# An adaLN transformer block: the gates go to rows through memory, and batch 1 is turned in periods 6 and 8

## The reference

```python
mod = (_silu(c) @ wmod).reshape(2, 6, 1, -1)
sa, ca, ga, sb, cb, gb = (mod[:, i] for i in range(6))
ga = (2 * (ga >= 0) - 1) * jnp.maximum(jnp.abs(ga), 0.25)
gb = (2 * (gb >= 0) - 1) * jnp.maximum(jnp.abs(gb), 0.25)
h = _layernorm(x) * (1 + ca) + sa
x = x + ga * attention(h)          # q, k, v; rope; causal softmax; Wo
h = _layernorm(x) * (1 + cb) + sb
x = x + gb * experts(h)            # top 2 of 8, rank-16 LoRA on w1, w3, w2
```

## Time and profile before

| | us |
|---|---|
| median of three runs | 471.87 (469.65 to 472.2) |
| time of the profiled execution | 469.36 |
| its span, first to last instruction | 467.6 |

### The profile page before, as it was taken

One profiled execution on the slowest core, in us unless ns is written; L12 is line 12 of the kernel. 1 busy time (PEld: TensorE's weight loads), 2 busy tenths in 40 slices (PEclk: granted clock), 3 DMA queues, 4 the chain that ended last, 5 costly groups with the idle time before them and its releaser, 6 DMA issues.

```text
span 467.6 us, 12314 instructions
## 1 busy us (share of the span) xinstructions
PE 438.4 (94%) x4511; PEld 314.3 (67%) x4511; DVE 364.2 (78%) x1004; ACT 349.1 (75%) x640; POOL 338.3 (72%) x287
## 2 busy tenths in 40 slices
PE   7978999989999999999999998988899997899995
PEld 4455776877877788787788876877765454454563
DVE  5975988888888789888889898988756669445576
ACT  3656999989899899989989889889626465653351
POOL 5448699996799976769999869935315875375792
PEclk8997999999999999999999999999999999999999
DMA  8347344765132774334357424491110000000001
GB/s 294 114 140 240 106 101 130 173 176 163 42 114 52 189 173 127 99 80 126 96 157 160 120 61 114 70 199 30 35 35 0 2 0 1 1 2 0 24 22 47
DMA packets 57948, 44.60 MB, mean 95 GB/s; under 512 B 36832, under 2 KB 49568, under 8 KB 57888
## 3 DMA queue, kind: packets, MB, share of 16 engines
q1 hardware_dynamic: 57472, 43.28, 34.8%
q10 hardware_dynamic: 416, 0.53, 0.3%
HBM read 23.41 MB, written 11.53 MB: 75 GB/s over the span
## 4 chain that ended last, share of the span: by engine, by line
PE 61%; ACT 12%; DVE 10%; POOL 8%; issue 6%; DMA 1%; ACTq 0%; DVEq 0%; POOLq 0%
PE ps L558 10%; PE ps L474 8%; PE ps L476 8%; PE ps L475 8%; PE ps L539 5%; PE ps L541 5%; PE ps L582 3%; ACT prob L962 3%; PE ps L586 3%; PE ps L584 3%; ACT ph L969 3%; PE ps L797 2%; PE ps L771 2%; DMA oT<-wmod 1%; POOL wst L1654 1%
## 5 line engine op out<-in xcount | busy, mean ns | idle before, releaser
L1306 DVE CUSTOM_DVE_ANT_0 prob<-ps,causal 128x512 f32<-128x512 f32 (+3 forms) x256 | 117.9, 485 | 11.5 <-PE ps L541 9.6
L962 ACT ACTIVATE prob<-prob,least 128x512 f32<-128x512 f32 (+3 forms) x256 | 122.6, 556 | 2.7 <-DVE least L1306 2.7
L1314 DVE SCALAR_TENSOR_TENSOR pl<-ps,ph 128x512 f16<-128x512 f32 (+1 forms) x128 | 105.1, 821 | 23.7 <-ACT ph L969 20.2
L969 ACT ACTIVATE ph<-ps 128x512 f16<-128x512 f32 (+1 forms) x128 | 87.1, 703 | 24.5 <-PE ps L558 21.9
L539 PE MATMUL ps<-kT_h,qT 128*128 128x512 f16 (+3 forms) x256 | 76.8, 302 | 7.9 <-DVE least L1306 5.4
L558 PE MATMUL ps<-ident,prob 128*128 128x128 f32 x640 | 82.6, 276 | 1.1 <-DVE pl L1314 0.6
L558 PEld LDWEIGHTS ps<-ident,prob 128*128 128x128 f32 x640 | 69.6, 142 | 2.4 <-DVE pl L1314 1.1
L541 PE MATMUL ps<-kT_l,qT 128*128 128x512 f16 (+3 forms) x256 | 70.4, 302 | 0.0
L582 PE MATMUL ps<-vh,ph 128*128 128x65 f16 x640 | 64.9, 194 | 2.5 <-ACT hT L913 1.2
L584 PE MATMUL ps<-vl,ph 128*128 128x64 f16 x640 | 64.9, 193 | 0.0
L586 PE MATMUL ps<-vh,pl 128*128 128x65 f16 x640 | 64.8, 193 | 0.0
(11 more groups left out here) (195 smaller groups left out, 1013.6 us busy)
## 6 DMA issues: line engine op xcount, KB each, us to landing
spill<-rot SPq DMA_DIRECT2D x20, 512.0 KB, 3.3
wst<-chunks SPq DMA_DIRECT2D x30, 256.0 KB, 4.2
qT<-spill SPq DMA_DIRECT2D x15, 512.0 KB, 3.6
kT_h<-spill SPq DMA_DIRECT2D x6, 256.0 KB, 4.1
xs<-x SPq DMA_DIRECT2D x2, 512.0 KB, 5.5
oT<-wmod SPq DMA_DIRECT2D x2, 512.0 KB, 8.8
raw<-chunks SPq DMA_DIRECT2D x4, 256.0 KB, 4.7
out<-xs SPq DMA_DIRECT2D x4, 256.0 KB, 2.1
```

The lines of the kernel that those rows point to most:

```text
L962: act.activation(prob[:, m % 2, c], prob[:, m % 2, c], ACT.Exp, bias=least[:, m % 2, qt:qt + 1], scale=-1.0).then_inc(exp_done, 1)
L969: act.activation(ph[:, m % 2, c], ps[:, PT_BANK:PT_BANK + 3, :].rearrange("p a b -> p (a b)")[:, c], ACT.Copy, scale=PROB_SCALE).then_inc( ...
L1306: ins = dve.tensor_tensor_reduce(prob[:, m % 2, at:at + w], ps[:, bank, off:off + w], causal[:, S - w:S], -1.0 / HD ** 0.5, 3.0e38, ALU.ad ...
L1314: dve.scalar_tensor_tensor(out=pl[:, m % 2, c], in0=ps[:, PT_BANK:PT_BANK + 3, :].rearrange("p a b -> p (a b)")[:, c], scalar=PROB_SCALE, ...
```

## The change

`XN2_AT` becomes `(6, 8)`. `modulate` for batch 1 leaves ScalarE; a `tensor_scalar` (multiply, then add) on VectorE stands in its place, at the end of the period. The gates no longer pass through TensorE and ScalarE: SyncE writes `g_abs` to a scratch tensor in memory, number by number, two periods ahead, and then reads each row back into all 128 partitions. `values` of periods 20 and 24 waits for the gates no longer; `residual_first` and `store_sum` wait for both transfers (a count of 32).

```diff
-XN2_AT, GATES_AT = (11, 13), (19, 23)
+XN2_AT, GATES_AT = (6, 8), (19, 23)
@@ SyncE, in the loop over periods
+                for i, at in enumerate(GATES_AT):
+                    if n == at - 2:
+                        sp.wait_ge(g_m, i + 1)
+                        for b in range(B):
+                            sp.dma_start(gate_rows[i, b].rearrange("(k p) -> p k", p=P), g_abs[:, 2 * i:2 * i + 2, b], allow_slow_non_contiguous=True)\
+                              .then_inc(g_written, 16)
+                    if n == at:
+                        sp.wait_ge(g_written, 16 * B * (i + 1))
+                        sp.dma_start(gates[:, B * i:B * (i + 1), :],
+                                     gate_rows[i].unsqueeze(0).broadcast_to([P, B, D])).then_inc(g_ready, 16)
@@ TensorE
-                if m - 1 in GATES_AT:
-                    pe.wait_ge(g_ready, GATES_AT.index(m - 1) + 1)
...
-                if n in GATES_AT:
-                    pe.wait_ge(normed, n + 1)
-                    gates_transposed(GATES_AT.index(n), PV_BANK)
@@ ScalarE
-                if n in XN2_AT:
-                    modulate(1, XN2_AT.index(n), PV_BANK)
                 if n - 1 in XN2_AT:
                     second_high(XN2_AT.index(n - 1))
-                if n + 1 in GATES_AT:
-                    gates_wide(GATES_AT.index(n + 1))
-                if n in GATES_AT:
-                    gates_out(GATES_AT.index(n), PV_BANK)
@@ VectorE, at the end of the period
+                if n in XN2_AT:
+                    k = XN2_AT.index(n)
+                    dve.wait_ge(xnT_mm, DK + k + 1)
+                    dve.wait_ge(hl_first, DK)
+                    dve.tensor_scalar(hT[:, k, :], ps[:, PV_BANK, :], modT[:, 2 + k, 1:2], modT[:, k, 1:2], ALU.mult, ALU.add)\
+                       .then_inc(hT_ready, 1)
@@ VectorE, store_sum
+                dve.wait_ge(g_ready, 32)
@@ GpSimd, residual_first
-                pool.wait_ge(g_ready, 1)
+                pool.wait_ge(g_ready, 32)
```

More of the change, by code:

```diff
@@ L128, in wait_apart, with block_kernel @@
     eng.sem_inc(passed, 1)
-def block_kernel(nc, x, chunks, cos, sin, cT, wmod, gateT, out, spill):
+def block_kernel(nc, x, chunks, cos, sin, cT, wmod, gateT, out, spill, gate_rows):
     ctx = ExitStack()
@@ L228, in chunk_space @@
             return flat.rearrange("p (a b) -> p a b", a=shape[1])
-        gwide, gwide2 = (chunk_space(w_h, FFN_CHUNK + 2 * i, [P, 4, P]) for i in range(2))
         wm = over(oT, [P, 3, DK, 512])
@@ L271, in block_kernel @@
         hl_first, hl_second = sem("hl_first"), sem("hl_second")
-        g_s, g_a, g_m, g_wide, g_mm, g_ready = (sem(f"g_{k}") for k in ("s", "a", "m", "wide", "mm", "ready"))
+        g_s, g_a, g_m, g_written, g_ready = (sem(f"g_{k}") for k in ("s", "a", "m", "written", "ready"))
         wh_ready, wl_ready = sem("wh_ready"), sem("wl_ready")
@@ L615, in _ @@
             modulation((8, 9), 1)
[L617 to L622, removed]
             def gate_logits(b):
@@ L1003, in _ @@
                 tile_out(i)
[L1005 to L1015, removed]
             def modulate_ffn(b, bank0, ks=range(DK)):
@@ L1837 @@
     spill = nc.dram_tensor("spill", (len(ITEMS), 4 * P, S), F16, kind="Internal").ap()
-    block_kernel(nc, *args, spill)
+    gate_rows = nc.dram_tensor("gate_rows", (2, B, D), F32, kind="Internal").ap()
+    block_kernel(nc, *args, spill, gate_rows)
     r = run_bass_kernel_spmd(nc, [arrays], core_ids=[0])
```

## The result

| | before | changed |
|---|---|---|
| median, us | 472.03 | 475.23 (473.5 to 476.24, 4 runs) |
| profiled execution, its time and span, us | 469.36, 467.6 | 473.5, 471.7 |
| ratio to before | | 1.0081, 95% interval 1.0054 to 1.0107 |

The change makes the kernel 0.8% slower, 3.8 us; 3.1 us less was forecast. The median of before counts a disturbed run of 749 us, which isn't in the ratio; without it the median is 471.87.

What follows compares the result with a forecast made beforehand. TensorE bounds the stage losing work, ScalarE with GpSimd the receiving one. -5.0 + 1.6 + 0.25 = -3.1 us: 466.3 us against the profiled execution, 468.8 against the median; 8-in-10 range 465.9 to 471.9.

Steps and rivals of the forecast that it cites:

- What bounds the two stages: TensorE bounds the stage losing work, period 12 being 1.91 us too long; ScalarE, with GpSimd beside it, bounds the receiving stage.
- What goes: Periods 11 to 14 lose transposes and TensorE stands, 2.8 us; periods 19 to 24 likewise, 2.1 us; together 5.0 us.
- What comes: Periods 7 to 9: moved work makes ScalarE 1.6 us late, derived through ScalarE with TensorE and through GpSimd; VectorE's modulate 0.
- The later wait of ScalarE for GpSimd: Near 103 us ScalarE stands 1.2 us for GpSimd's late rotation; 0.25 us of it reaches TensorE at period 14.
- SyncE and the transfers: Second pair of small writes, issued near 151.2 us: a landing of up to 9.9 us costs nothing; 0 us taken.
- The prediction's own signs of being wrong: ph of head 11 over 3 us later; TensorE waiting for hT in period 7 or 9, or a transfer behind period 19.
- the queue rival: SyncE's queue: writes landing after 20 us hold what is queued behind them, costing 6.6 us, 475.4 us in all; chance 0.04.

Runs made afterwards that it cites:

- turn_only: The kernel before with only batch 1's turn moved to periods 6 and 8 with VectorE's modulate, gates still through TensorE; 0.9967 of before.
- second_late: The changed kernel with the second pair of gate rows written in period 56 and read back in period 58; 1.0031 of before.
- second_end: The changed kernel with the second pair of gate rows written behind the last transposing transfers, after the loop, and read back at once; 0.9937 of before.
- gates_only: The changed kernel with batch 1 turned in periods 11 and 13 with ScalarE's modulate, as before; 1.0117 of before.
- writes_added: The kernel before plus only the second pair of 4-byte writes (512 numbers) in period 21, read back by nobody; 1.0103 of before.
- second_end_again: second_end run again, unchanged, on the same chip as three other kernels; 0.9943 of before.

## Why the prediction was wrong, point by point

- *What bounds the two stages*: right. The windows and the `norm` distances were the views to read.
- *What goes*, 5.0 us: right. Periods 19 to 24 gave 2.08 us (2.1 priced); periods 11 to 15 gave 1.46 + 1.12 = 2.6 us (2.8 less 0.25), and 2.75 in turn_only, second_late and second_end. Of the excess of 1.91 us read in period 12, 0.15 was this execution's own: gates_only and writes_added, unchanged there, have 6.15 us where 6.30 stood.
- *What comes*, 1.6 us by two ways: right, 1.63 us at `norm` of periods 10 and 11. VectorE's `modulate` is listed with 0.80 us where 0.69 was taken from line 1279, and cost nothing visible.
- *The later wait of ScalarE for GpSimd*: right as a wait, 1.15 us where 1.2 was derived. That 0.25 us of it reaches TensorE is borne out by the changed kernel at best (0.2); with the 2.75 us above nothing of it is left in the others. The turn as a whole was forecast at -2.8 + 1.6 + 0.25 = -0.95 us and is -0.95 in the changed kernel and -1.1 in turn_only.
- *SyncE and the transfers*: this step failed, and alone turned -3.1 into +3.8 us. That a landing of up to 9.9 us costs nothing had two faults. The size: I took 3.3 us from a spill of 512 KB, and the pair took 13.2 us. And the test, which by what follows would have misled at a shorter landing as well (argued, no run has one): I looked for what SyncE's *wait* holds up, the instruction behind it in the queue. But the writes slow every transfer that is in flight with them, from the spill issued 0.4 us earlier on. The one that mattered was the query fetch. Against second_end, which has the same turn and no writes here, it was late twice over: it waits for the spill, which took 7.2 us and not 3.1, and so was issued 2.2 us later (4.99 us behind `norm` of period 23, and 2.81), and it landed 6.2 us later behind its issue (10.4 us, and 4.2). Of these 8.4 us its user had 2.9 to spare (in second_end it landed at 160.6 us and TensorE began with it at 163.50), which leaves the stand of 5.4 but for rounding. The slack that had to be read was that from each transfer's landing to its first user, not the queue's. The prediction's own signs of being wrong named both, a landing past 9.9 us and a wait of TensorE for a transfer behind period 19.
- *The rivals*: the queue rival, at 0.04, gave the time (475.4) by another mechanism; its condition (landing past 16.5 us) didn't hold, so the agreement is luck. The rule of the Trainium skill that I set aside ("DMA: Bandwidth & Descriptors", Specifications: below 512 bytes a transfer reads, modifies and writes) was the warning; the prediction gave a slow landing 0.04 in all. The runs agree with it in part: 4-byte pieces are slow when side by side (13.1 us), and about as fast as others when apart (3.7 us), where the rule would make both slow.
- *The forecast of the whole* stands for the change without its second pair of writes in period 21: second_end is at 0.9937 and second_end_again at 0.9943, -3.0 and -2.7 us.

## What to carry to other kernels

A transfer that is cheap in bytes can still hold up all others in flight: look for its landing time in a row of the same shape, and where there is none, treat the price as open and give it a rival with a real chance. Judge a slow transfer by everything in flight beside it, and by how much later each of those could land before its user wants it; a stage that moves almost no bytes may still have a transfer on the path. If numbers must be spread element by element, do it where nothing else is wanted, which second_end shows; keeping neighbouring elements apart in memory, or writing pieces of 16 bytes, did no harm in one execution each.

## What the runs showed of the hardware

- 512 writes of 4 bytes to neighbouring places in HBM from 128 partitions took 9.3 us alone (second_end) and 11.4 to 13.9 us among others (second_late, writes_added, the changed kernel, gates_only); at 512 bytes' distance 3.7 us; 256 pieces of 16 bytes 4.6 us; to on-chip memory 2.9 us. Alone, their packets were through within 2 us, and the rest of the 9.3 us shows no packet on any transfer engine.
- Transfers issued just before or behind the adjacent 4-byte writes landed after 7.2 to 13.3 us in the changed kernel; before, those of the same kinds between 118 and 180 us took 2.4 to 5.4 us.
- In TensorE's stand of 5.4 us the granted clock fell to its lower level and stayed there for the first 3.6 us of work behind it (0.50), which made the stand a third dearer (7.4 us). In second_late, behind a stand of 3.6 us, the grant was still 1.00 when TensorE went on (321.45 us) and 0.57 from 322 to 326 us.
- Executions differ by up to 3.2 us before period 3. Behind it, kernels that are alike differ by up to 0.5 us up to period 21 and by 0.02 us between periods 28 and 45, if no transfer comes late: the trace tells differences of 1 us that a median of six runs hardly does.
